# Causal attention in units of four heads by 512 queries, with the mask of the row maxima added in the DVE instruction that takes the maximum

## What is computed

```python
scores = jnp.einsum('bqhd,bkhd->bhqk', q, k) / jnp.sqrt(jnp.float32(D))
causal = jnp.tril(jnp.ones((T, T), dtype=bool))
scores = jnp.where(causal, scores, jnp.float32(-1e+30))
p = jax.nn.softmax(scores, axis=-1)
y = jnp.einsum('bhqk,bkhd->bqhd', p, v).reshape(B, T, C)
```

## Time and profile before

| | us |
|---|---|
| median of 3 runs | 3068.51 |
| lowest and highest run | 3059.32, 3070.42 |
| span of the profiled execution, from the first to the last instruction | 3064.6 |
| attention stages in it | 89.5 to 678.1, 1353.4 to 1929.3, 2287.3 to 2862.2 |
| PE busy | 2459.5 (80%) |
| DVE busy | 1968.9 (64%) |
| ACT busy | 1467.3 (48%) |

### The profile page before, as it was taken

The page is one execution under the profiler, slowest core; times in us unless marked ns, Lnnn a source line. Parts: engine busy times, 40 slices in busy tenths (PEclk is TensorE's granted clock), DMA queues, the critical chain, the costliest instruction groups (busy, mean ns, idle before and its releaser), DMA issues. The chain is left out here.

```text
span 3064.6 us, 68154 instructions
## 1 busy us (share of the span) xinstructions
PE 2459.5 (80%) x23684; PEld 1331.0 (43%) x23684; DVE 1968.9 (64%) x4246; ACT 1467.3 (48%) x2102; POOL 542.6 (18%) x1023
## 2 busy tenths in 40 slices
PE   3698998994699538648998999897138899999898
PEld 2244444453344325424444444565123444444565
DVE  6576676757477774567777776334957677777333
ACT  3254455564599545334555555323233555555422
POOL 4011111111244315140111111000340111111100
PEclk7699999996799768869999999999668999999899
DMA  3101110000111000010010000000011000010000
GB/s 105 71 33 37 38 38 34 33 10 0 57 48 49 12 0 1 0 65 32 33 40 36 31 31 24 1 0 0 0 50 44 35 31 31 38 40 23 1 1 14
DMA packets 45622, 89.65 MB, mean 29 GB/s; under 512 B 9104, under 2 KB 27792, under 8 KB 45456
## 3 DMA queue, kind: packets, MB, share of 16 engines
q1 hardware_dynamic: 45456, 87.34, 7.8%
HBM read 73.29 MB, written 13.63 MB: 28 GB/s over the span
## 5 line engine op out<-in xcount | busy, mean ns | idle before, releaser
L1021 DVE TENSOR_REDUCE max_part<-stat 128x1 f32<-128x512 f32 (+3 forms) x1968 | 1074.9, 595 | 407.8 <-PE stat L902 203.0
L884 ACT ACTIVATE probs<-score 128x1024 f32<-128x1024 f32 (+1 forms) x960 | 859.5, 896 | 807.0 <-PE score L924 804.7
L934 PE MATMUL pv<-probs,v_head 128*32 128x128 f32 x13056 | 635.4, 285 | 0.5 <-POOL probs L854 0.5
L924 PE MATMUL score<-q_exp,k_exp 128*128 128x512 bf16 (+3 forms) x1920 | 536.5, 363 | 121.0 <-DMA q_exp<-row_max_turned 100.0
L902 PE MATMUL stat<-k_max,q_max 128*128 128x512 bf16 (+3 forms) x1968 | 581.7, 365 | 64.0 <-DMA k_max<-k_parts 48.4
L934 PEld LDWEIGHTS pv<-probs,v_head 128*32 128x32 f32 x13056 | 367.7, 111 | 301.7 <-issue 279.8
L902 PEld LDWEIGHTS stat<-k_max,q_max 128*128 128x128 bf16 x1968 | 162.0, 100 | 324.2 <-DVE max_part L1021 131.5
L833 POOL COPY v_head<-qkv 128x16 f32 (+2 forms) x258 | 51.1, 199 | 1191.1 <-ACT probs L884 1190.4
L924 PEld LDWEIGHTS score<-q_exp,k_exp 128*128 128x128 bf16 x1920 | 140.9, 98 | 276.3 <-issue 209.4
L1978 ACT ACTIVATE gate<-gate_ps 128x512 f32<-128x512 f32 x128 | 76.4, 597 | 264.0 <-PE gate_ps L1953 264.0
L854 POOL TENSOR_SCALAR_AFFINE_SELECT probs<-probs 128x256 f32<-128x256 f32 x384 | 155.9, 406 | 251.4 <-ACT probs L884 251.2
(11 more groups left out here) (268 smaller groups left out, 2569.8 us busy)
## 6 DMA issues: line engine op xcount, KB each, us to landing
q_max<-q_parts SPq DMA_DIRECT2D x192, 96.0 KB
k_max<-k_parts SPq DMA_DIRECT2D x192, 96.0 KB
q_exp<-q_parts SPq DMA_DIRECT2D x144, 96.0 KB
k_exp<-k_parts SPq DMA_DIRECT2D x144, 96.0 KB
q_parts<-parts_t SPq DMA_DIRECT2D x16, 384.0 KB, 2.6
k_parts<-parts_t SPq DMA_DIRECT2D x16, 384.0 KB, 3.3
q_exp<-row_max_turned SPq DMA_DIRECT2D x192, 1.0 KB
expert_wv<-in_L_ffn_expert_wv SPq DMA_DIRECT2D x1, 2048.0 KB, 8.5
```

The source lines that it names most:

```text
L884: nc.scalar.activation(probs[:, e % PSLOTS, 0:width], sc[e % 2][:, 0:width], ACT.Exp, scale=scale).then_inc(expd.sem, 1)
L924: last = nc.tensor.matmul(out, ke[:, par, kt * P:(kt + 1) * P], qe[:, par, j * BANK + f * P:(j + 1) * BANK], start=True, stop=True)
L934: last = nc.tensor.matmul(acc[32 * c:32 * c + 32, j * P:(j + 1) * P], vh[:, par, kt, :], probs[:, e % PSLOTS, at:at + P], start=kt == 0, s ...
L1021: nc.vector.reduce_max(mpart[:, par, i, col:col + 1], ring[at % RING][:, 0:width], AX.X).then_inc(stat_used.sem, 1)
```

## The change

`attention_stage` is written anew, and the code around it is adapted. The work of a stage is cut into 16 units, each of four heads by 512 queries (`UNITS`: group of heads, block of queries j). A unit has 4(j+1) steps of one key tile each, 160 steps in all. `attention_plan` sets where in these steps the maxima, the transposes of the row maxima (`shift`) and those of the results (`out`) stand; `RING` is that list, and it is the same one for PE and DVE.

- **A step t on PE** is: wait for the first exponential of t, two score matmuls of t+1 (heads 0 and 1), ring items, the V matmuls of t-1, wait for the second exponential of t, two score matmuls of t+1 (heads 2 and 3), ring items. The V matmuls are four, one for each head on a column group of its own, with 9 weight columns (V and a column of ones) and up to 512 query columns; the trace of before has no record of that shape.
- **The maxima** of a unit are 16(j+1) pieces, 640 a stage, of which 256 hold the diagonal (128, 256, 384 or 512 keys wide, 64 of each). For those the mask matmul is gone, and DVE adds a mask row from SBUF and takes the maximum in one `tensor_tensor_reduce`, which writes the sum and an accumulator.
- **Loads.** One buffer of q and k serves both the maxima and the scores; there are three such buffers. `load(u)` is 24 DMAs: for each of four heads and three parts, one of k (24 rows of 512(j+1) keys) and one of q (24 rows of 512 queries). `load(u+3)` goes out when the scores of the last step of unit u are made. At the start SP issues `load(0)`, twelve small DMAs that set the rows of -1, `load(1)`, `load(2)` and the first row maxima. The rows of row maxima go in two DMAs per unit.
- **The rest.** PE reads 72 partitions for a maximum and 74 for a score, instead of 128. POOL no longer gathers V: ACT copies it once per stage into an array with ones. All loops over heads are unrolled. Memsets of the load stage are fewer, `q_exp` and `k_exp` are gone from it, and the result of a stage goes over the q part of `qkv`.

```diff
+HG = 4
+NG = H // HG
+BUFS = 3
+UNITS = [(0, 0), (0, 1), (0, 2), (0, 3), (1, 3), (2, 3), (3, 3), (1, 2), (2, 2), (3, 2), (1, 1), (1, 0), (2, 1), (2, 0), (3, 1), (3, 0)]
...
+        maxima = [("max", u, (h, s, c)) for s in range(QC) for c in range(j + 1) for h in range(HG)]
...
+        due.append((len(stream) + LATE + 1, max(1, first[u] - 3) if u else 0))
...
+    free = [min(first[u - BUFS + 1] + 3, first[u - 1] - 2) if u >= BUFS else -1 for u in range(len(UNITS))]
...
+                    if u >= BUFS:
+                        sp.wait_ge(scored.sem, scored.at(2 * LAST[u - BUFS] + 2))
+                    keys = BANK * (j + 1)
+                    for h in range(HG):
+                        for a in range(PARTS):
+                            at = slice(a * PARTS * D, (a + 1) * PARTS * D)
+                            sp.dma_start(uk[at, b, h, 0:keys], k_rows[g * HG + h][:, :, 0:keys]).then_inc(loaded[b].sem, 16)
...
+                load(0)
+                sp.wait_ge(minus_ready.sem, minus_ready.at(1))
...
+                load(1)
+                load(2)
+                load_shift(0)
+                for u in range(NU):
+                    if u + 1 < NU:
+                        load_shift(u + 1)
+                    if u + BUFS < NU:
+                        load(u + BUFS)
...
-                    if own:
-                        last = nc.tensor.matmul(out[:, width - P:width], w["ident16"][:], w["mask16"][:], start=False, stop=True)
...
+                        if kind == "max" and arg == (0, 0, 0):
+                            pe.wait_ge(loaded[u % BUFS].sem, loaded[u % BUFS].at(loads_of(u)))
...
+                    if hp == 0 and t == FIRST[u]:
+                        pe.wait_ge(shift_in.sem, shift_in.at(SHIFT * 16 * (u + 1)))
...
+                    for h in range(HG):
+                        last = nc.tensor.matmul(acc[32 * h:32 * h + D + 1, f:BANK], v9[:, kt, g * HG + h, :], probs[:, (2 * t + h // 2) % PSLOTS, h % 2, 0:BANK - f],
+                                                start=kt == 0, stop=kt == QC * j + QC - 1, tile_position=(0, 32 * h))
...
-                    nc.vector.reduce_max(mpart[:, par, i, col:col + 1], ring[at % RING][:, 0:width], AX.X).then_inc(stat_used.sem, 1)
...
+                        nc.vector.tensor_tensor_reduce(masked[:, at % 2, 0:width], ring[n % RBANKS][:, 0:width], w["mask_row"][:, BANK - width:BANK], 1.0, NEG,
+                                                       ALU.add, ALU.max, accum_out=into).then_inc(stat_used.sem, 1)
+                    else:
+                        nc.vector.reduce_max(into, ring[n % RBANKS][:], AX.X).then_inc(stat_used.sem, 1)
```

More of the change, by code:

```diff
@@ L682, in attention_stage @@
+LATE = 3
 def attention_stage(k, w, v, parts_dram, scale, y):
     nc = k.nc
[L694 to L705, removed]
@@ L895, in _ @@
+                copy_out(NU - 1)
             @block.tensor
             def _(pe):
-                def max_unit(n, unit, par):
-                    i, at, width, _ = MAXU[unit]
-                    out = ring[n % RING]
-                    own = at + width > i * P
-                    last = nc.tensor.matmul(out[:, 0:width], qm[:, par, i * P:(i + 1) * P],
-                                            km[:, par, at:at + width], start=True, stop=not own)
-                    if own:
-                        last = nc.tensor.matmul(out[:, width - P:width], w["ident16"][:], w["mask16"][:], start=False, stop=True)
-                    last.then_inc(stat_full.sem, 1)
@@ L1000, in _, with max_unit @@
-                body(0, 0, 0, plan=HEAD0_PLAN)
-                with pe.Fori(0, H // 2 - 1) as i:
-                    body(2 * i + 1, i, 1)
-                    body(2 * i + 2, i + 1, 0)
-                body(H - 1, H // 2 - 1, 1, plan=LAST_PLAN)
+                def max_unit(n, u, h, s, c):
+                    g, j = UNITS[u]
+                    b = u % BUFS
+                    own = c == j
+                    width = (s + 1) * P if own else BANK
+                    out = ring[n % RBANKS]
+                    last = nc.tensor.matmul(out[:, 0:width], uq[0:KROWS, b, h, s * P:(s + 1) * P], uk[0:KROWS, b, h, c * BANK:c * BANK + width],
+                                            start=True, stop=True)
+                    last.then_inc(stat_full.sem, 1)
@@ new lines, in scores @@
+                def scores(t, hp):
+                    u, kt = STEPS[t]
+                    b, f = u % BUFS, first_col(t)
+                    if hp == 0 and t == FIRST[u]:
+                        pe.wait_ge(shift_in.sem, shift_in.at(SHIFT * 16 * (u + 1)))
+                    for i in range(2):
+                        h = 2 * hp + i
+                        last = nc.tensor.matmul(sc[hp][:, i, 0:BANK - f], uk[0:ROWS, b, h, kt * P:(kt + 1) * P], uq[0:ROWS, b, h, f:BANK],
+                                                start=True, stop=True)
+                    last.then_inc(scored.sem, 1)
```

557 lines of the change are left out of this document (230 added, 327 removed).

## The result

| | us |
|---|---|
| before, median | 3069.47 |
| changed, median of 4 runs (3173.75 to 3192.26) | 3180.76 |
| ratio, 95% interval | 1.0373, 1.0344 to 1.0402 |

What follows compares the result with a forecast made beforehand. PE was taken to bound the kernel before; in the changed one, SP-issued loads stall it. 584.5 + 16 = 600 us a stage; 1325.2 + 3 x 600 = 3125 us span, plus 3.9: 3129 us, range 3000 to 3220.

Steps and rivals of the forecast that it cites:

- Seven waits for the loads of units 9 to 15: Last 45% of a stage: PE stands 5 to 13 us at each first maximum until its load lands, about 63 us.
- The load: Unit load: 24 DMAs at 0.744 us of SP issue, 0.4 for the last, about 2 to land: 20.3 us.
- The start: Stage start: first score 65 us in, against 36.9 before, behind three unit loads, twelve small DMAs and the row maxima.
- The full step: PE's step of four scores, four maxima and V of four heads: 2.80 us, against 3.10 for the same work before.
- The rival of a bounding DVE in full steps: Full steps: a step over 2.9 us, DVE bounding, would show the forecast wrong; no chance given.
- V on nine columns: V matmuls: taken as side by side, 0.86 us for four; rival not side by side, 2.6 us more a step, chance 0.01.
- DVE: DVE's busy time per stage: 384 to 405 us, with 0.10 to 0.19 us per accumulator read, under PE's 400 to 450.
- The clock term: Eight stalls a stage, each followed by 3.5 us at 0.53 clock, about 2 us lost each: 16 us.
- Steps 0 to 23: Stage's first steps: 20 us for step 0, 75 for steps 1 to 23, about 5 waiting for `load(3)`; step 24 at 165.
- From step 86 on: Stage's last part: seven chained loads, 142 us, plus 104.5 us of work between a landing and the next departure.
- The closing balance: Per stage: gains of 48 and 33 us against costs of 28 at the start, about 33 dense maxima, about 63 stalls.
- The faster rival: Unit loads: SP issues the narrower loads faster, at 0.45 us, and the stalls go; 2913 us in all, chance 0.25.

Runs made afterwards that it cites:

- the run without late loads: Changed kernel with SP's loads stopped after unit 5, units 6 to 15 computing on what lies in their buffers; 2940.4 us, 0.9582.
- the run with the mask by matmul: Changed kernel with the causal mask of the row maxima again added by matmul and all maxima plain reductions; 3169.4 us, 1.0327.
- the run whose clock was at 1.00 there: Kernel with loads on SP and POOL queues and mask by matmul, plus extra matmuls before the first score and in step 0; 2856.5 us, 0.9329.
- the three kernels with a cheaper or a shared issue: Changed kernel with q loads issued by POOL, 2959.2 us; with 18 DMAs of 8 rows per unit, 2978.0; with both and fewer DMAs for rows of -1, 2879.8.
- the 18-DMA kernel: Changed kernel with each unit load as 18 DMAs of 8 rows by four heads instead of 24 of 24 rows by one head; 2978.0 us, 0.9708.

## Why the prediction was right, and where it was off

- **Direction and cause** stand. Seven waits for the loads of units 9 to 15 were forecast at 5 to 13 us, some 63 in a stage. The first stage has 4.6, 3.3, 10.1, 11.7, 11.7, 1.1 and 11.8 us, together 54.3, with three of them under 5.
- **The load** (24 x 0.744 + 2.4 = 20.3 us) is measured: 556.64 to 577.23, 20.6.
- **The start** (65 us) is 65.5, 65.3 and 66.0 us in the three stages.
- **The full step** (2.80 us) is 2.78: 63 steps, from the scores of step 24 to those of step 87, take 175.4 us in the first stage. The rival of a bounding DVE in full steps is out. V on nine columns runs side by side.
- **DVE** was put at 384 to 405 us, and is 370: the accumulator read costs 0.084 us, below the 0.10 to 0.19 that I took from ACT's. By the sum's own terms the lower end is 382 (230 + 103 + 26 + 23), and with 0.084 it is 378; the other 8 us stay open. It was right that a read exists and that the two-input instruction isn't slower.
- **The clock term was mis-sized**, 16 us a stage for eight waits. The last part alone loses 27 us by it (the run without late loads), and the first steps 8 to 14 more. I took 3.5 us at half clock behind each wait from the earlier trace rows. Behind the wait for unit 13, which ends at 611.57, it is 21 us:

```profile
611.60:633.00 21.40, 20.70 (x84) 6.51 (x85) 8.40 (x39) 8.92 (x10) 0.41 (x1) 0.50 0.13 39
```

  And behind the long wait of the start the clock is low for most of the way to step 8:

```profile
173.00:195.00 22.00, 21.64 (x85) 5.75 (x83) 15.36 (x38) 7.67 (x10) 1.63 (x4) 0.50 0.11 38
```

- **Steps 0 to 23** were forecast at 100 us from the first score to step 24, and take 107, 112 and 114. Step 0 was right (the scores of step 2 follow the first by 20.1 us). The 5 us of waiting for `load(3)` didn't come in any stage: the steps before it, at half clock, took longer than the load. In the run with the mask by matmul, whose clock was at 0.89 from step 2 to step 8 in the first stage, they were shorter, and PE waited 2.1 us for it. So 12 to 19 us came from elsewhere. 8 to 14 of them are the clock, and 4 in each stage stay open. Steps 2 to 8 take 29.4, 31.2 and 31.5 us, against 21.8 in the run whose clock was at 1.00 there (its mask is by matmul); steps 12 to 24 take 41.9 us at 1.00 in the first stage and 45.5 and 46.4 in the others. For this the sum had no term. With 7 to 14 us more a stage it would have come to some 3160.
- **From step 87 on** the sum had 244 us (246 from step 86) and 16 for the clock, and the first stage has 266 (434.8 to 700.7). That it is off by 6 only is luck, for two errors nearly cancel: the waits' idle time is 54 instead of 63 us, and the clock's part 27 instead of 16. They aren't independent. Slow steps hide a load: between the waits for units 13 and 14 the steps take 22 us at 0.50, and the second wait is 1.1 us; in the run with the mask by matmul they take 15 us at 0.85, and it is 8.0.
- **Slips in the working that the total doesn't feel.** The time to move the bytes of a load of 2048 keys, 12 x (1.25 + 0.31), is 19 us and not 22. DVE's lower end is 382, not 384. The cover of units 12 and 13, given as 3 and 0 steps, is 4 and 3 by the plan. The closing balance, 81 us gained against 124 lost, makes 43 a stage where the sum itself has 20.
- **The faster rival** fell on its condition: the 24-row DMA's issue time doesn't depend on its bytes. That another form has 0.30 us, and that a second queue helps, is what the runs added: the rival's figure of 2913 for a short issue lies among the 2880 to 2978 of the three kernels with a cheaper or a shared issue.

## What to carry to other kernels

When a tiling is made finer, count the DMAs of a unit and multiply by the issue time of their form: 24 x 0.74 us had to fit under 3 to 6 steps of 2.8 us, and did not. Ask of every load which bound holds it, the issuing engine or the queue's rate. Here it is told by the time from the end of the last issue to the moment at which the waiting engine goes on: 2.7 us in the changed kernel, where SP's issue bounds, and 9.4 in the 18-DMA kernel, where the queue does (524.4 to 533.8). The cure is different: fewer or cheaper DMAs and a second issuer for the one, a second queue for the other. And price an idle gap of TensorE with the stretch behind it: 27 us beside 51 of idle time in the last part of a stage here. When two variants differ by a few us in a stretch, look at its granted clock before the difference is put down to an instruction.

## What the runs showed of the hardware

- The issue of a DMA costs SP 0.70 us for 24 rows that come as three by eight, for rows of 1 KB and of 4 KB alike, and 0.27 to 0.30 us for 8 rows, be it of one head or of four. POOL needs 0.60 and 0.54.
- With more issued than it had landed, one queue moved 78 GB/s at a DMA share of 0.20 (24-row loads, the kernel before) and 62 at a share of 0.55 (8-row loads, one queue); SP's and POOL's queues together moved 133 at 0.64 (8-row loads).
- The two-input maximum with an accumulator is as fast per column as the plain reduction, 692 against 687 ns for 512 columns, and its accumulator read is 84 ns.
- Ten us of matmuls brought the clock to 1.00, and it was back at 0.50 after 5.9 us without work, at the first score. With 12 extra matmuls before the first score and 66 inside step 0 it was at 1.00 from step 2 to step 8, where it is 0.61 without them.
